# Flamingo attention and feed-forward block: the last query stack issued behind both sums, and the opening's splits and transfers put in another order

## The chip, the cores and the metric

The kernel runs on 1 core of one Trainium2 chip. Its time is the device time of one execution in microseconds (us), as the median of several runs. A core has five engines that run their own instruction streams in order: TensorE (PE, with its weight loads as PEld), VectorE (DVE), ScalarE (ACT), GpSimd (POOL) and SyncE (SP), which only issues transfers here. ACT issues transfers too, from the same stream as its computations. Semaphores are all that couples the streams.

## The reference, cut to what matters

64 sequences of 256 positions and 512 features, each on its own:

```python
def _L0_xattn_ref(q, k, v, ffn_w, ffn_b):      # q = layernorm(x), k = v = ctx
    qs = relu(q.reshape(bs, ts, 16, 32)); ks = relu(k...); vs = relu(v...)
    att = einsum('bthf,byhf->bhty', qs, ks)
    att = softmax(att / sqrt(32), axis=-1)
    out = einsum('bhty,byhf->bhtf', att, vs).reshape(bs, ts, -1)
    return relu(out @ ffn_w.T + ffn_b)
# _L0_ffn_ref: xr, xk mix x with x of the position before (mu_r, mu_k);
#   r = sigmoid(xr @ W_r); out = r * (square(relu(xk @ W_k)) @ W_v)
x = x + tanh(g_xattn) * _L0_xattn_ref(layernorm(x), ctx, ctx, ffn_w, ffn_b)
x = x + tanh(g_ffn)   * _L0_ffn_ref(layernorm(x), W_r, W_k, W_v, mu_r, mu_k)
```

## The kernel before

The 16 heads of a sequence are four groups c = 0 to 3 of four heads. Products are taken in fp32r from high and low halves: a value is split into a rounded part (ACT, `q_halve` L598, `k_halve` L603) and the rest (DVE, `q_low` L838, `k_low` L844). The halves of the queries and keys go to memory (`write_q` L558 on ACT's queue, `write_k` L263 on SP's) and come back stacked on 96 partitions, group by group (`stack_q` L573 on ACT, `stack_k` L283 on SP). A group's heads can be multiplied once both stacks have landed.

For each head PE makes `scores` (L1079, from which DVE takes the row maximum, `head_max` L858) and, with the maxima moved into a 97th row of `q_st` (`move_m` L295), `shifted_scores` (L1095), whose exponent ACT takes (`exponent` L618). For group 1 alone the denominators are not made by PE: ACT sums the exponents of the plain scores in the score bank itself (`sum_exp` L621, heads 4 to 7), and PE may write the next scores to that bank only behind it: `scores` of heads 7, 8 and 9 of a sequence wait for the sums of heads 5, 6 and 7. The attention output goes to memory (`write_o` L303) and back in another layout (`read_o` L309, tile `o_mv`, in two halves for each of two position tiles u); ACT and POOL split it (`o_high` L635, `o_low` L431) and PE multiplies it (`project` L1151). That is done for tile 0 at the end of an iteration, and for tile 1 in the next one.

Each engine has a function `iteration(i, par)` that writes out its order by hand: in iteration i the heads of sequence i, the projection and feed-forward layers of i-1 and i-2 between them, and the preparation of i+1 and i+2. `pipeline` runs i = -3 to 3 unrolled, a loop of two iterations a turn, and the last ones unrolled. Iterations -2, -1 and 0 of SP have an order of their own, `opening` (L330), since nothing is in the pipeline yet. There the weights are loaded and split as well. Sequence 0 has its group 0 written to memory by itself (`k_first`, `q_first`), so that its stack need not wait for the rest.

In ACT's `iteration` (L705) the second line is `stack_q(i, 3, par)`, behind `exponent(i, 0)` and ahead of `sum_exp(i, 6)`.

## Time and profile before

| | |
|---|---|
| median of 3 runs | 2684.31 us |
| lowest, highest | 2683.58, 2691.25 us |
| the profiled execution's own time | 2686.47 us |
| its span, first to last instruction | 2684.7 us |
| PE busy | 2597.9 us, 97% of the span |
| DVE, ACT, POOL busy | 85%, 63%, 43% |

So 1.77 us of the profiled execution lie outside its span. The page gives for each group of instructions its busy time, and the time its engine sat idle just before it with the one that ended that idle time (`<-`). Idle time of an engine that is not the bottleneck costs nothing. The span divides into an opening of some 130 us, 61 or so sequences at an even pace of about 40.4 us, and an ending.

### The profile page before, as it was taken

How to read it: one execution, taken by the hardware profiler on the slowest of the kernel's cores; microseconds unless marked ns; L12 is line 12 of the kernel's file. 1: busy time of each engine (PE TensorE's matmuls, PEld its weight loads, DVE VectorE, ACT ScalarE, POOL GpSimd, SP SyncE). 2: the span in 40 equal slices, each digit the busy share in tenths (PEclk: the TensorE clock that was granted, in tenths of full speed). 3: DMA queues.
4: the chain of work that ended last, by engine and by line, in shares of the span. 5: the costliest groups of instructions: out<-in, count | busy, mean ns of one | idle time of the engine just before them, and what ended most of it. 6: DMA issues, size and time to landing. Idle time of an engine off the chain costs nothing. (4 is left out here: it accounts for less than half of the span.)

```text
span 2684.7 us, 66755 instructions
## 1 busy us (share of the span) xinstructions
PE 2597.9 (97%) x20354; PEld 2074.9 (77%) x20354; DVE 2282.9 (85%) x4109; ACT 1695.4 (63%) x3531; POOL 1162.9 (43%) x902
## 2 busy tenths in 40 slices
PE   3799999999999999999999999999999999999998
PEld 2577778787787787787787778778778778787776
DVE  6688888888888889888888888888888888888875
ACT  4466666666666666666666666666666666666663
POOL 0144444444444444444444444444444444444434
PEclk9799999999999999999999999999999999999999
DMA  9787777777777778778778778787787787777751
GB/s 256 210 215 228 215 213 230 222 212 229 221 209 233 223 208 234 218 209 234 223 209 234 218 211 232 211 222 224 214 227 222 211 231 222 211 228 220 209 153 44
DMA packets 523216, 576.78 MB, mean 215 GB/s; under 512 B 191264, under 2 KB 422688, under 8 KB 523168
## 3 DMA queue, kind: packets, MB, share of 16 engines
q1 hardware_dynamic: 369648, 340.71, 46.5%
q10 hardware_dynamic: 153520, 235.46, 30.1%
q8 instruction: 26, 0.43, 0.1%
q14 instruction: 22, 0.18, 0.0%
HBM read 373.56 MB, written 201.33 MB: 214 GB/s over the span
## 5 line engine op out<-in xcount | busy, mean ns | idle before, releaser
L618 ACT ACTIVATE probs<-bank 128x512 f32<-128x512 f32 x1024 | 610.2, 596 | 523.2 <-PE bank L1103 519.7
L858 DVE TENSOR_REDUCE m_nat<-bank 128x2 fp32r<-128x512 f32 x1024 | 689.2, 681 | 76.5 <-PE bank L1091 76.3
L1091 PE MATMUL bank<-k_st,q_st 96*128 96x256 f32 x2048 | 435.1, 295 | 37.5 <-ACT bank L630 26.2
L877 DVE RECIPROCAL o_val<-bank 128x256 f32<-128x256 f32 x192 | 336.7, 1754 | 138.8 <-PE bank L1129 138.8
L1091 PEld LDWEIGHTS bank<-k_st,q_st 96*128 96x128 f32 x2048 | 362.8, 193 | 108.0 <-ACT bank L630 40.1
L1103 PE MATMUL bank<-q_st,k_st 97*128 97x256 f32 x2048 | 426.2, 290 | 8.6 <-DMA q_st<-m_t 8.2
L1103 PEld LDWEIGHTS bank<-q_st,k_st 97*128 97x128 f32 x2048 | 357.3, 191 | 85.5 <-issue 23.3
L464 POOL TENSOR_TENSOR xm<-xm 128x512 f32<-128x512 f32 x128 | 157.1, 1227 | 463.0 <-ACT xm L677 462.0
L630 ACT ACTIVATE bank<-bank,m_nat 128x256 f32<-128x256 f32 x512 | 227.6, 444 | 136.5 <-DVE m_nat L858 136.2
L431 POOL TENSOR_TENSOR o_lo<-o_mv,o_hi 128x512 fp32r<-128x512 f32 x128 | 168.6, 1317 | 304.5 <-ACT o_hi L640 302.1
L1146 PE MATMUL bank<-xk_hi,w_hi 128*128 128x256 f32 x1024 | 294.9, 288 | 1.0 <-DVE th L940 1.0
L1146 PE MATMUL bank<-xk_hi,w_lo 128*128 128x256 f32 x1024 | 288.3, 282 | 0.0
L1146 PE MATMUL bank<-xk_lo,w_hi 128*128 128x256 f32 x1024 | 288.1, 281 | 0.0
L1117 PE MATMUL bank<-probs,v_pos 128*32 128x256 f32 x4096 | 278.1, 390 | 0.0
L449 POOL TENSOR_TENSOR xk_lo<-xm,xk_hi 128x512 fp32r<-128x512 f32 x128 | 209.3, 1636 | 125.3 <-DVE xm L923 111.6
L423 POOL TENSOR_TENSOR rstd<-ve,mhalf 128x1 f32<-128x1 f32 x128 | 69.4, 542 | 415.2 <-DVE ve L907 415.2
L1146 PE MATMUL bank<-w_hi,o_hi 128*128 128x512 f32 x512 | 208.7, 408 | 2.3 <-POOL o_lo L431 2.1
L1146 PE MATMUL bank<-w_hi,xr_hi 128*128 128x512 f32 x512 | 207.9, 406 | 0.0
L1146 PE MATMUL bank<-w_hi,ka_hi 128*128 128x512 f32 x512 | 206.9, 404 | 0.0
L1129 PE MATMUL bank<-probs,ones_r 128*32 128x256 f32 x3072 | 203.6, 383 | 0.0
L1146 PE MATMUL bank<-w_lo,o_hi 128*128 128x512 f32 x512 | 203.2, 397 | 0.0
L1146 PE MATMUL bank<-w_hi,ka_lo 128*128 128x512 f32 x512 | 202.0, 394 | 0.0
(94 smaller groups left out, 5945.8 us busy)
## 6 DMA issues: line engine op xcount, KB each, us to landing
q_st<-q_dram ACTq DMA_DIRECT2D x256, 256.0 KB, 4.8
k_st<-k_dram SPq DMA_DIRECT2D x256, 256.0 KB, 4.7
k_raw<-ctx_t_dram SPq DMA_DIRECT2D x256, 128.0 KB, 5.1
q_st<-q_dram ACTq DMA_DIRECT2D x256, 128.0 KB, 2.9
k_st<-k_dram SPq DMA_DIRECT2D x256, 128.0 KB, 5.0
o_dram<-o_val SPq DMA_DIRECT2D x256, 128.0 KB, 2.1
o_mv<-o_dram SPq DMA_DIRECT2D x1024, 32.0 KB, 3.1
x<-x_dram ACTq DMA_DIRECT2D x64, 512.0 KB, 6.7
```

The costliest lines, as they stand in the source:

```text
L431: nc.gpsimd.tensor_tensor(by_tile(o_lo, u), o_mv[:, :, :].rearrange("p g (k a) -> p k g a", k=KC), by_tile(o_hi, u).bitcast(F32), ALU.subt ...
L449: nc.gpsimd.tensor_tensor(xk_lo[:, part, :], xm[:, part, :], xk_hi[:, part, :].bitcast(F32), ALU.subtract).then_inc(xk_lo_ready, 1)
L464: nc.gpsimd.tensor_tensor(part, part, part, ALU.mult).then_inc(ka_ready, 1)
L618: nc.scalar.activation(probs[:, n // GR % 2, n % GR, :, :].rearrange("p v t -> p (v t)"), st_bank[n % 2][:, :], ACT.Exp).then_inc(exp_read ...
L630: last = nc.scalar.activation(scores, scores, ACT.Exp, bias=m_nat[:, SUMMED % 2, g, u:u + 1].bitcast(F32), accum_out=den[:, NU * g + u:NU ...
L858: nc.vector.tensor_reduce(m_nat[:, c % 2, n % GR, :], s_bank[n % 2][:, :].rearrange("p (u y) -> p u y", u=NU), AX_X, ALU.max, negate=True) ...
L877: nc.vector.reciprocal(o_val[:, c % 2, :], pv_bank[:, T:2 * T]).then_inc(rden_ready, 1)
L1091: mm = nc.tensor.matmul(s_bank[n % 2][:, T * u:T * u + T], q_st[0:QK, c, g, P * u:P * u + P], k_st[0:QK, c, g, :], start=True, stop=True)
L1103: mm = nc.tensor.matmul(st_bank[n % 2][:, T * v:T * v + T], k_st[0:ST, c, g, P * v:P * v + P], q_st[0:ST, c, g, :], start=True, stop=True)
L1117: nc.tensor.matmul(pv_bank[HD * g:HD * g + HD, 0:T], v_pos[:, v, HD * h:HD * h + HD], probs[:, c % 2, g, v, :], start=(v == 0), stop=(v == ...
L1129: mm = nc.tensor.matmul(pv_bank[HD * g:HD * g + HD, T:2 * T], ones_r[:, 0:HD].bitcast(F32), moving, start=(n == 0), stop=(n == len(sums) - 1))
L1146: mm = nc.tensor.matmul(dst, lhs[a], rhs[c], start=first and n == 0, stop=last and n == 2, skip_group_check=True)
```

## The change

1. **All sequences.** `stack_q(i, 3)`, two transfers, moves on ACT from ahead of `sum_exp(i, 6)` to behind `sum_exp(i, 7)`.
2. **Sequence 0, splits.** The keys are split before the queries; the queries of group 0 are split in instructions of their own, and written as soon as these are through.
3. **Sequence 1, splits.** `k_halve(1)` moves from ACT's iteration -1 to iteration 0, behind `sum_exp(0, 6)`; `k_low(1)` on DVE to behind `head_max(0, 9)`.
4. **SP's opening.** Key writes and stacks move ahead of loads; the reads of `o_mv` are spread out, the second one ahead of `move_m(1, 0)`.

```diff
@@ SP: opening
                 if i == -2:
                     load_k(0)
                     load_w(range(0, 4))
+                    write_k_first(0, par)
                     load_x(1)
+                    stack_k(0, 0, par)
                     write_k(0, par)
                 elif i == -1:
-                    stack_k(0, 0, 1 - par)
                     stack_k(0, 1, 1 - par)
+                    stack_k(0, 2, 1 - par)
+                    move_m(0, 0)
                     load_k(1)
-                    move_m(0, 0)
-                    stack_k(0, 2, 1 - par)
                     load_x(2)
...
                     stack_k(1, 0, 1 - par)
+                    stack_k(1, 1, 1 - par)
                     load_k(2)
                     move_m(0, 3)
                     load_w(range(6, 7))
                     write_o(0, 0)
-                    stack_k(1, 1, 1 - par)
                     load_x(3)
+                    read_o(0, 0, 0)
                     write_o(0, 1)
                     stack_k(1, 2, 1 - par)
+                    read_o(0, 0, 1)
                     move_m(1, 0)
                     load_w(range(7, 8))
-                    read_o(0, 0, 0)
-                    read_o(0, 0, 1)
@@ ACT: write_q, sequence 0
+                        act.wait_ge(q_hi_first, 1)
+                        act.wait_ge(q_lo_first, 1)
                         for half, tile in enumerate((q_high, q_raw)):
                             act.dma_start(q_dram[par, 0, half].rearrange("f g t -> (f g) t"),
                                           tile[:, 0, :]).then_inc(q_first, 16)
+                    act.wait_ge(q_hi_ready, b + 1)
+                    act.wait_ge(q_lo_ready, b + 1)
@@ ACT: iteration
+                if isinstance(i, int) and i == -2:
+                    k_halve(i + 2)
...
                 exponent(i, 0)
-                stack_q(i, 3, par)
                 sum_exp(i, 6)
+                if isinstance(i, int) and i == 0:
+                    k_halve(i + 1)

                 exponent(i, 1)
                 split_high(i, 6, 1)
                 sum_exp(i, 7)
+                stack_q(i, 3, par)
@@ DVE: iteration
                 head_max(i, 9)
+                if isinstance(i, int) and i == 0:
+                    k_low(i + 1)
                 stats_1(i + 2)
...
                 norm_1(i + 2)
+                if isinstance(i, int) and i == -2:
+                    k_low(i + 2)
```

What this does to the streams, at three places. ACT in iteration 1 and all later ones, before: the two transfers `q_st<-q_dram` of group 3 stand behind the first exponent (L618), ahead of the sums (L630) of heads 6 and 7; after them L677 clears a bank.

```order
L640 ACTIVATE o_hi<-o_mv 128x4x128
L630 ACTIVATE bank,den<-bank,m_nat 128x256 x2
L618 ACTIVATE probs<-bank 128x512
L580 DMA q_st<-q_dram 32x1024
L581 DMA q_st<-q_dram 64x1024
L630 ACTIVATE bank,den<-bank,m_nat 128x256 x2
L618 ACTIVATE probs<-bank 128x512
L630 ACTIVATE bank,den<-bank,m_nat 128x256 x2
L618 ACTIVATE probs<-bank 128x512
```

The same stretch of ACT now:

```order
L653 ACTIVATE o_hi<-o_mv 128x4x128
L643 ACTIVATE bank,den<-bank,m_nat 128x256 x2
L631 ACTIVATE probs<-bank 128x512
L643 ACTIVATE bank,den<-bank,m_nat 128x256 x2
L631 ACTIVATE probs<-bank 128x512
L643 ACTIVATE bank,den<-bank,m_nat 128x256 x2
L587 DMA q_st<-q_dram 32x1024
L588 DMA q_st<-q_dram 64x1024
L631 ACTIVATE probs<-bank 128x512
```

Both transfers moved past two sums and one exponent. SP at the end of its opening, before, from the weights `th` on (L300 moves the maxima, L307 writes the attention output, L315 reads it back, eight transfers in one go):

```order
L241 DMA th<-w_v_dram 128x2x512
L307 DMA o_dram<-o_val 128x256
L289 DMA k_st<-k_dram 64x1024
L291 DMA k_st<-k_dram 32x1024
L252 DMA x_ln<-x_dram 16x2x512 x8
L307 DMA o_dram<-o_val 128x256
L289 DMA k_st<-k_dram 64x1024
L291 DMA k_st<-k_dram 32x1024
L300 DMA q_st<-m_t 1x8x128
L241 DMA xn<-w_v_dram 128x2x512
L315 DMA o_mv<-o_dram 32x4x64 x8
```

The same stretch of SP now:

```order
L243 DMA th<-w_v_dram 128x2x512
L311 DMA o_dram<-o_val 128x256
L254 DMA x_ln<-x_dram 16x2x512 x8
L319 DMA o_mv<-o_dram 32x4x64 x4
L311 DMA o_dram<-o_val 128x256
L295 DMA k_st<-k_dram 64x1024
L297 DMA k_st<-k_dram 32x1024
L319 DMA o_mv<-o_dram 32x4x64 x4
L304 DMA q_st<-m_t 1x8x128
L243 DMA xn<-w_v_dram 128x2x512
```

The key stack of sequence 1, group 1, left this stretch for an earlier place, and all of `o_mv` now stands ahead of the maxima's row `q_st<-m_t`. SP at its start, before, from the key load of sequence 0 on:

```order
L260 DMA k_raw<-ctx_t_dram 32x4x256 x4
L241 DMA probs<-w_x_dram 128x2x512 x2
L241 DMA x<-w_r_dram 128x2x512 x2
L252 DMA x_ln<-x_dram 16x2x512 x8
L272 DMA k_dram<-k_high 128x256
L272 DMA k_dram<-k_raw 128x256
L275 DMA k_dram<-k_high 128x3x256
L275 DMA k_dram<-k_raw 128x3x256
L289 DMA k_st<-k_dram 64x1024
L291 DMA k_st<-k_dram 32x1024
```

The same stretch of SP now:

```order
L262 DMA k_raw<-ctx_t_dram 32x4x256 x4
L243 DMA probs<-w_x_dram 128x2x512 x2
L243 DMA x<-w_r_dram 128x2x512 x2
L279 DMA k_dram<-k_high 128x256
L279 DMA k_dram<-k_raw 128x256
L254 DMA x_ln<-x_dram 16x2x512 x8
L295 DMA k_st<-k_dram 64x1024
L297 DMA k_st<-k_dram 32x1024
L271 DMA k_dram<-k_high 128x3x256
L271 DMA k_dram<-k_raw 128x3x256
```

Group 0 of the keys goes out ahead of the load of x of sequence 1 (`x_ln`), and is stacked ahead of the other groups' writes.

## Rows read from the trace of the kernel before

**Rows 1.** The page: span, and its section 1, busy us, share, instructions.

```profile
span 2684.7 us, 66755 instructions
...
PE 2597.9 (97%) x20354; PEld 2074.9 (77%) x20354; DVE 2282.9 (85%) x4109; ACT 1695.4 (63%) x3531; POOL 1162.9 (43%) x902
```

**Rows 2.** Waits of PE, 140 to 2600 us: us in total, times, longest.

```profile
PE bank L1091 <- ACT bank L630: 15.9, 61, 0.3
...
PE bank L1146 <- POOL o_lo L431: 0.5, 1, 0.5
```

**Rows 3.** Timeline, one sequence: start, us, engine, line, op, out<-in, shapes, [idle<-releaser].

```profile
1014.84 0.44 ACT L630 ACTIVATE bank<-bank,m_nat 128x256 f32<-128x256 f32 x1
...
1015.86 0.36 ACTq L580 DMA_DIRECT2D q_st<-q_dram  x1
...
1015.91 0.50 PE L1091 MATMUL bank<-k_st,q_st 96*128 96x256 f32 x2 [0.26 <-ACT bank L630]
...
1016.88 0.45 ACT L630 ACTIVATE bank<-bank,m_nat 128x256 f32<-128x256 f32 x1 [0.51 <-DVE m_nat L858]
...
1020.78 0.40 PE L1091 MATMUL bank<-k_st,q_st 96*128 96x256 f32 x2
...
1021.57 0.21 ACT L630 ACTIVATION_READ_ACCUMULATOR bank<-bank,m_nat 128x1 f32 x1
...
1021.97 0.41 PE L1091 MATMUL bank<-k_st,q_st 96*128 96x256 f32 x2
```

**Rows 4.** The output write at 1021.5: duration ns, start; its landing, us.

```profile
L307 SPq DMA_DIRECT2D o_dram<-o_val x1: 344/344/344, 1021.5 to 1021.5; - x1
...
DMA to landing us min/median/max: 1.7/1.7/1.7
```

**Rows 5.** The output write at 101.3, issued among a query stack's two transfers.

```profile
L307 SPq DMA_DIRECT2D o_dram<-o_val x1: 343/343/343, 101.3 to 101.3; - x1
...
DMA to landing us min/median/max: 2.3/2.3/2.3
```

**Rows 6.** Stretch: us, PE, PEld, DVE, ACT, POOL busy, PEclk, DMA share, GB/s.

```profile
1021.00:1024.00 3.00, 3.00 (x27) 3.00 (x26) 2.98 (x8) 2.47 (x7) 0.67 (x1) 1.00 0.35 96
1024.00:1029.00 5.00, 5.00 (x34) 4.57 (x33) 4.70 (x12) 3.13 (x5) 2.48 (x3) 1.00 0.89 270
```

**Rows 7.** Timeline of POOL and PE at the projection of tile 1, two sequences.

```profile
1030.30 1.44 POOL L431 TENSOR_TENSOR o_lo<-o_mv,o_hi 128x512 fp32r<-128x512 f32 x1 [1.58 <-ACT o_hi L640]
...
1032.23 0.48 PE L1146 MATMUL bank<-w_hi,o_hi 128*128 128x512 f32 x1
...
1353.94 1.28 POOL L431 TENSOR_TENSOR o_lo<-o_mv,o_hi 128x512 fp32r<-128x512 f32 x1 [1.75 <-ACT o_hi L640]
...
1355.37 0.47 PE L1146 MATMUL bank<-w_hi,o_hi 128*128 128x512 f32 x1
```

**Rows 8.** Timeline of the opening, sequence 0: ACT and PE.

```profile
14.07 1.04 ACT L607 ACTIVATE k_high<-k_raw 128x1024 fp32r<-128x1024 f32 x1
...
28.06 1.19 PE L1091 MATMUL bank<-k_st,q_st 96*128 96x256 f32 x4 [2.99 <-DMA k_st<-k_dram]
...
37.06 0.80 PE L1091 MATMUL bank<-k_st,q_st 96*128 96x256 f32 x2 [4.20 <-ACT bank L630]
...
47.75 0.80 PE L1103 MATMUL bank<-q_st,k_st 97*128 97x256 f32 x2 [2.17 <-DMA q_st<-m_t]
```

**Rows 9.** Timeline of the opening, start of sequence 1: PE and ACT.

```profile
68.39 0.77 PE L1091 MATMUL bank<-k_st,q_st 96*128 96x256 f32 x2 [4.57 <-DMA k_st<-k_dram]
...
76.37 0.80 PE L1103 MATMUL bank<-q_st,k_st 97*128 97x256 f32 x2 [2.55 <-DMA q_st<-m_t]
76.97 1.05 PE L1042 MATMUL bank<-w_hi,ident_r 128*128 128x512 f32 x2
...
79.63 0.63 ACT L640 ACTIVATE o_hi<-o_mv 128x512 fp32r<-128x512 f32 x1 [5.40 <-DMA o_mv<-o_dram]
...
81.22 0.80 PE L1091 MATMUL bank<-k_st,q_st 96*128 96x256 f32 x2 [3.20 <-ACT bank L630]
```

**Rows 10.** Timeline of SP's issues in the same stretch.

```profile
61.74 0.52 SPq L289 DMA_DIRECT2D k_st<-k_dram  x1
...
62.95 5.37 SPq L252 DMA_DIRECT2D x_ln<-x_dram  x8
...
73.14 0.69 SPq L300 DMA_DIRECT2D q_st<-m_t  x1
...
74.35 3.79 SPq L315 DMA_DIRECT2D o_mv<-o_dram  x8
```

More of the change, by code:

```diff
@@ L145, in flamingo_block @@
         q_copied = sem("q_copied")
+        q_hi_first = sem("q_hi_first")
+        q_lo_first = sem("q_lo_first")
         q_first = sem("q_first")
@@ L266, in write_k @@
                     sp.wait_ge(k_lo_ready, b + 1)
-                    groups = slice(0, CH)
-                    if first_sequence(b):
-                        groups = slice(1, CH)
-                        for half, tile in enumerate((k_high, k_raw)):
-                            sp.dma_start(k_dram[par, 0, half].rearrange("f g t -> (f g) t"),
-                                         tile[:, 0, :]).then_inc(k_first, 16)
+                    groups = slice(1 if first_sequence(b) else 0, CH)
                     for half, tile in enumerate((k_high, k_raw)):
@@ L276, in write_k, with write_k_first @@
                                      tile[:, groups, :]).then_inc(k_written, 16)
+            def write_k_first(b, par):
+                sp.wait_ge(k_hi_ready, b + 1)
+                sp.wait_ge(k_lo_ready, b + 1)
+                for half, tile in enumerate((k_high, k_raw)):
+                    sp.dma_start(k_dram[par, 0, half].rearrange("f g t -> (f g) t"),
+                                 tile[:, 0, :]).then_inc(k_first, 16)
             def keys_written(b):
@@ L288, in stack_k @@
                         sp.wait_ge(k_first, 32)
+                    if first_sequence(b) and c == 1:
+                        sp.wait_ge(k_written, 32)
                     sp.dma_start(k_st[0:2 * HD, c, :, :].bitcast(F32),
@@ L291, in stack_k @@
                     sp.dma_start(k_st[2 * HD:QK, c, :, :].bitcast(F32), k_dram[par, c, 0]).then_inc(k_stacked[c], 16)
-                    if first_sequence(b) and c == 0:
-                        sp.wait_ge(k_written, 32)
             def move_m(b, c):
@@ L600, in q_halve @@
                     act.wait_ge(q_copied, NU * (b + 1))
-                    nc.scalar.activation(q_high[:, :, :].bitcast(F32R), q_raw[:, :, :], ACT.Copy).then_inc(q_hi_ready, 1)
+                    groups = slice(0, CH)
+                    if first_sequence(b):
+                        groups = slice(1, CH)
+                        nc.scalar.activation(q_high[:, 0, :].bitcast(F32R), q_raw[:, 0, :],
+                                             ACT.Copy).then_inc(q_hi_first, 1)
+                    nc.scalar.activation(q_high[:, groups, :].bitcast(F32R), q_raw[:, groups, :],
+                                         ACT.Copy).then_inc(q_hi_ready, 1)
             def k_halve(b):
@@ L762, in iteration @@
                 xt_copy(i - 1, 1)
-                k_halve(i + 2)
+                if not (isinstance(i, int) and i < 0):
+                    k_halve(i + 2)
                 exponent(i, 11)
@@ L1005, in iteration @@
                     q_low(i + 2)
-                k_low(i + 2)
+                if not (isinstance(i, int) and i < 0):
+                    k_low(i + 2)
                 split_low(i, 4, 0)
```

12 lines of the change are left out of this document (8 added, 4 removed).

## The prediction

> **What bounds the kernel now.** I read the page first: the span is 2684.7 us and PE is busy for 2597.9 us of it, 97% [rows 1]. PE is the bound, so an edit counts only where it moves PE. Next the waits of PE over the even-paced part, 140 to 2600 us. Only one group is of note: 61 waits, one a sequence, for a sum on ACT, 15.9 us together or 0.26 us each; the projection waits for POOL once in all that time [rows 2]. So the even-paced part has at most some 16 us to give, and only if the edit touches that one wait. The rest of PE's idle time lies in the opening, where single waits reach 4.57 us [rows 8, 9]. I followed both places in the timeline.
>
> **The wait in the loop, and which sum it is.** The reader is to match the two L630 stretches of one sequence with PE. The sum at 1014.84 is head 5's, ahead of the exponent; PE's scores of head 7 start at 1015.91 as it ends, with the 0.26 us of idle time. The query stack is issued at 1015.86, behind it. The sum that follows the stack, head 6's, starts at 1016.88, and what waits for it (scores of head 8) runs at 1020.78, 2.9 us after that sum is through (1016.88 plus twice 0.45, and its readout). Head 7's sum ends at 1021.78 (1021.57 + 0.21) and head 9's scores start at 1021.97; but this sum stands behind exponent 1, which waits for PE itself, not behind the stack [rows 3]. So the moved stack blocked none of PE's waits: its two issues cost ACT some 0.3 us ahead of head 6's sum, all of it covered by 2.9 us. **Gain of the move in the loop: 0.** That the 15.9 us stay is my first claim.
>
> **What the moved stack now meets.** It is issued about 5.5 us later, at about 1021.4 instead of 1015.86, while head 7's sum runs [rows 3]. On ACT the two issues (0.36 us and about 0.5 us) run beside that sum's tail; the exponent of head 2 behind them comes at most 0.5 us later, and PE asks for it only two heads on. Its landing has room: group 3 is not multiplied until head 12, three heads behind head 9's scores. Cost on ACT: 0. But in memory traffic it now falls beside the write of the attention output of group 3, issued at 1021.5. That write begins a chain: it lands in 1.7 us [rows 4], `o_mv` is read back, ACT makes `o_hi`, POOL `o_lo`, PE projects. In the sequence shown POOL is through at 1031.74 (1030.30 + 1.44) and PE projects at 1032.23, a room of 0.49 us. In another it is through at 1355.22 and PE projects at 1355.37: 0.15 us is the signal alone, there is no room [rows 7]. Over the 59 sequences that I measured so, 9 have no room, the median is 0.66 us. A delay of the last `o_mv` by d costs PE what is left of d: summed over these rooms (less the 0.15 us), 0.3 us of delay would cost some 3.5 us in all, 0.5 us some 9 us, 0.8 us some 19 us.
>
> How large is d? The nearest row from above is the same write at 101.3, issued among the two transfers of a query stack: 2.3 us instead of 1.7 [rows 5], 0.6 us late. From below: the traffic has a hole just there, a DMA share of 0.35 in 1021 to 1024, 1.95 us of free time, against 0.89 behind it [rows 6]. The stack's 393 kB need 1.3 us at the 303 GB/s of a full share (270 GB/s at 0.89); so it fits, and adds nothing, if it falls well. SP has the output of x to issue before it reads `o_mv` back, which hides another 0.1 to 0.2 us of the write. I take d = 0.2 us, nearer to the hole, since the end of the chain hangs on the traffic of 1024 to 1029, which the hole shields: 9 sequences at 0.2 us, and 0.3 us from the rest: **+2.1 us**. The ends are 0 and +9 us (d = 0.5).
>
> On this the Trainium skill has a rule that speaks against the change: DMA: Bandwidth & Descriptors, section Queues, rings and completion order, says that each DMA engine takes turns between the queues that have work, a packet at a time. By that rule the stack on ACT's queue would take every second turn from the write on SP's and slow it as in rows 5; by the hole it would not. It is the second rival below.
>
> **The opening, step by step.** It is a row of gates; a gain ahead of a gate counts only if the gate moves too.
> First gate: group 0 of sequence 0 is multiplied at 28.06, when the key stack lands. The keys were split last, at 14.07 and without any wait for them [rows 8]; now they are split while ACT and DVE wait for x, so the write goes out some 5 us sooner, and the stack lands 4 to 6 us sooner. The query side comes 1.5 us sooner too, by the short first split (a quarter of the elements). Price: x of sequence 1 is loaded 2 us later and its query copy stands ahead of the stack of queries of group 1, so group 1 wins 1 us at most. PE's wait at 37.06 for a sum (4.20 us) came from the splits of sequence 1's keys on ACT and DVE; both are gone from there: about 2.5 us sooner.
> Second gate, 47.75: the maxima's row of group 1 [rows 8]. On SP it stands behind the load of x of sequence 2, and that behind the key load, which now is issued later. I find it 0.5 to 1 us sooner; 1.5 to 2 us of the win are lost. The later `k_low(1)` moves the writes of sequence 1's keys by at most 1 us either way.
> Third: 68.39, 4.57 us of waiting for the key stack of group 1, issued at 61.74 [rows 9, 10]. It now stands right behind group 0's, 6 us sooner. This wait goes, 4 us. What is late next is the gate at 76.37, the maxima's row issued at 73.14. SP's queue before it, from 61.7: 5.4 for x (without the stack ahead of it it starts 1.2 us sooner), 1.9 for four `o_mv` issues (half of 3.79), 0.4 and 1.1 for write and stack, then the second read has to wait for the write issued at about 69.0 to land (1.7 us in the loop [rows 4]; up to 6 us in this traffic, in which the stack of 61.74 was needed at 68.39 and had not come before), and 1.9 for its four issues: 72.6 to 76.9, against 73.14. I take 3 us for the landing, 73.9 in all: this gate is 0.8 us *later*, at 77.2, and the 4 us are lost.
> Fourth: 81.22, PE waits 3.20 us for a sum, which stood behind `o_high`, which waited for `o_mv` until 79.63 [rows 9]. The reads end with SP at 72.6 to 76.9 instead of 78.14 (74.35 + 3.79), so this is 1.2 to 5.5 us sooner and with the 73.9 no longer binds; what does is PE itself: 77.2 plus 1.7 us (76.37 to 78.02, the two L1042 products included) is 78.9. **So the opening gives 81.22 - 78.9 = 2.3 us; with the earlier signals a little more, -2.5 us.** Ends: the row of maxima could be late by 3.8 us, which turns the gain into a loss of 0.7 us, or early by 0.5 us, which gives 3.6 us; to that up to 1 us either way for what the first gates hand on: +1 to -5 us. Behind 81.22 the order is the old one and I expect the gain to be carried to the end, since PE works without a break from 130 us on.
>
> **Sum**, against the span of 2684.7 us: -2.5 + 2.1 = -0.4, 2684.3 us. The profiled execution took 2686.47 us, 2.2 above the median of 2684.31. On the median it is 2684.31 - 0.4 = **2683.9 us**. About 0.3%, 8 us, is what a measurement of this kernel can tell from no change.
>
> **Rivals.**
> 1. *The chain to the projection breaks in most sequences (slower).* The stack takes the place in the traffic that `o_mv` had, d = 0.8 us or more; PE then waits at L1146 for POOL in 35 or more of 61 sequences: +19 us at 0.8 us, +27 at 1.0. With the opening 2684.3 - 2.5 + 19 = 2701. For it: ACT waits for `o_mv` in every sequence already. Against it: the hole of 1.95 us [rows 6]. It decides from d = 0.6 us on. Chance 0.10.
> 2. *The two queues take turns.* The write lands 0.6 us late as in rows 5, SP's other issue hides 0.1 us, d = 0.5 us: 2684.3 + 8.7 - 2.5 = 2690.5. The skill's rule of turns, named above, is this case. Chance 0.17.
> 3. *The opening gives nothing.* The maxima's row of sequence 1 is the gate and comes 2 us or more late, since two reads now stand before it. With the 2.1 us: 2686.4. Chance 0.17.
> 4. *The opening's gains carry through*: the gate at 76.37 does not come later, and the 3.20 us, the 4.57 us and 2 us from the first gates are all kept: 2684.3 - 9.8 = 2674.5. Against it: SP's queue. Chance 0.11.
> 5. The forecast, 2681 to 2686: chance 0.45.
>
> **Numbers.** The range has to leave out no more than 2 in 10: from 2678, which cuts most of rival 4, to 2693, which takes in rival 2 with 3 us above it and leaves rival 1. Faster by over 0.3% is below 2676.3: most of rival 4, 0.09. Slower is above 2692.4: rival 1 and a quarter of rival 2, 0.14. The rest, 0.77, is within.
>
> **What the profile after would show.** Right: 61 waits of PE for ACT's sums, 16 us in all, as before; waits of L1146 for POOL in about ten sequences, 1 to 4 us in all; the opening with no wait near 68 us, one near 73 to 77 us for the row of maxima of 3 us or more, and the third `exponent` stage some 2.5 us sooner. Wrong: if the 15.9 us shrink, my reading of which sum PE waits for is false; if waits at L1146 come to 8 us or more, d is mis-sized; if sequence 2 starts more than 5 us or less than 0 us sooner, my SP queue is.

## The result: slower, and the profile after

Seven runs of each kernel on one chip: the changed kernel 2697.49 us (2692.67 to 2701.94), the kernel before 2688.44 us (2679.15 to 2693.47). The ratio is 1.0038, 95% interval 1.002 to 1.0055: **slower by 0.4%, some 10 us of 2688** (9.1 us between the medians), where I had forecast no change, 2683.9 us, and a range that ended at 2693. The forecast was wrong, and what happened is its first rival. On another chip the same kernel gave 2695.77 against 2685.3, ratio 1.003 (1.0018 to 1.0043).

The page after: span and the busy lines of section 1, to be set against [rows 1].

```profile
span 2700.2 us, 66759 instructions
...
PE 2601.9 (96%) x20354; PEld 2076.5 (77%) x20354; DVE 2282.7 (85%) x4110; ACT 1689.4 (63%) x3532; POOL 1156.6 (43%) x902
```

PE has the same 20354 products and 4 us more of busy time in a span 15.5 us longer. So it waits more. These are two single executions, 15.5 us apart where the medians are 9.1 apart; a part of the difference is explained below. The waits of PE from 140 to 2600 us (us in total, times, longest), against [rows 2]:

```profile
PE bank L1120 <- ACT bank L643: 15.5, 60, 0.3
PE bank L1175 <- POOL o_lo L436: 12.5, 24, 1.1
PE bank L1132 <- DMA q_st<-m_t: 0.8, 1, 0.8
```

The first line is the wait that a reader would have wanted the move to shorten. It was 15.9 us in 61 waits and is 15.5 in 60: untouched. The second was 0.5 us, once; now the projection waits for POOL in 24 sequences. Of the waits before, one line of the same view did not stand ahead of the prediction, and matters now: PE's turning of the maxima (L1058) waited for DVE.

```profile
PE bank L1058 <- DVE m_t L867: 4.5, 9, 0.6
```

After, that line is gone: as I read it, a PE that has just waited for POOL finds the maxima ready. So 12.0 us came in and 4.5 us were given back. All lines of this view together are 21.3 us before and 29.0 after, +7.7 us. DVE takes the reciprocals of a sequence's first denominators once a sequence (tile `rden`), and I use the start of that as the sequence's mark: from mark 3 to mark 60 the kernel before takes 2308.5 us, the changed one 2318.8, +10.3 us. The opening, up to mark 3, is 0.9 us longer, the rest behind mark 60 is 4.2 us longer.

Two parts of this are not waits in that view. Between the marks PE's busy time is 2.9 us longer (2288.4 and 2291.3 us), with the same 18127 products at the full clock; what draws it out is not shown. And behind mark 60 most of the 4.2 us is the clock's. The columns of this row are those of [rows 6]; PEclk, the third number from the end, is the granted clock, and 0.50 is the lower of PE's two levels, 1.2 GHz.

```profile
2658.50:2665.30 6.80, 6.19 (x15) 4.87 (x16) 4.40 (x7) 1.76 (x5) 3.33 (x3) 0.50 0.00 0
```

PE had stood idle for 3.27 us, until 2659.11, waiting for POOL's half of the output, and the clock fell in that wait. Products of 512 columns then follow each other at 0.43 us, and at 0.24 once the clock is back, so PE's 6.19 us there cost some 2.8 us, an estimate. The wait itself is 1.7 us longer than the longest for POOL in the ending before (1.6 us). The profile before has no such stretch until its last 1.1 us, behind PE's last product, and the second profile of the changed kernel, on the other chip (span 2694.7 us), none behind mark 60 until its last 0.2 us.

**The chain that now sets PE.** ACT and its queue (ACTq) in the sequence that answers to [rows 3]; columns are start, duration, engine, line, operation, out<-in, and in brackets the idle time ahead and its releaser. The exponent of head 1 is L631, the sums are L643, the moved stack L587 and L588.

```profile
1025.26 0.60 ACT L631 ACTIVATE probs<-bank 128x512 f32<-128x512 f32 x1 [2.71 <-PE bank L1132]
1025.52 0.33 ACTq L587 DMA_DIRECT2D q_st<-q_dram  x1
1025.75 0.45 ACT L643 ACTIVATE bank<-bank,m_nat 128x256 f32<-128x256 f32 x1
1025.88 0.51 ACTq L588 DMA_DIRECT2D q_st<-q_dram  x1
```

The stack stands behind the sum of head 7 in the code, yet its first transfer is issued 0.23 us before that sum starts, while the exponent of head 1 still runs. SP's queue in the same sequence, and the landing of its output write (to be set against [rows 4]):

```profile
1026.45 0.34 SPq L311 DMA_DIRECT2D o_dram<-o_val  x1
...
1029.72 1.85 SPq L319 DMA_DIRECT2D o_mv<-o_dram  x4
```

```profile
L311 SPq DMA_DIRECT2D o_dram<-o_val x1: 343/343/343, 1026.5 to 1026.5; - x1
...
DMA to landing us min/median/max: 3.2/3.2/3.2
```

So the stack goes out 0.93 us *ahead* of the write, whose landing takes 3.2 us instead of 1.7, and the read, which waits for that landing, is issued 3.27 us behind the write. What follows, on ACT, POOL and PE, against [rows 7]:

```profile
1035.86 0.63 ACT L653 ACTIVATE o_hi<-o_mv 128x512 fp32r<-128x512 f32 x1 [2.17 <-DMA o_mv<-o_dram]
...
1036.57 1.27 POOL L436 TENSOR_TENSOR o_lo<-o_mv,o_hi 128x512 fp32r<-128x512 f32 x1 [2.39 <-ACT o_hi L653]
...
1037.99 0.47 PE L1175 MATMUL bank<-w_hi,o_hi 128*128 128x512 f32 x1 [0.71 <-POOL o_lo L436]
```

ACT stands idle for 2.17 us until `o_mv` is there, POOL's second half is through at 1037.84, and PE, 0.71 us idle, starts 0.15 us behind it, which is the signal alone. The traffic shows the same: the hole of [rows 6], a DMA share of 0.35 in the 3 us up to the read of the tile, is filled to 0.71 (us, busy time of PE, PEld, DVE, ACT, POOL, then the granted clock, the DMA share, GB/s):

```profile
1026.00:1029.00 3.00, 3.00 (x27) 3.00 (x26) 3.00 (x8) 2.46 (x7) 0.68 (x1) 1.00 0.71 187
1029.00:1034.00 5.00, 5.00 (x34) 4.57 (x33) 4.70 (x13) 3.13 (x5) 2.32 (x3) 1.00 0.83 260
```

The trace also records the packets of each queue: their number, MB, and share of the 16 engines' time. In the sequence above, 1027 to 1028 has packets of ACT's queue (q10) alone, though SP's write was issued at 1026.45; in 1028 to 1029 both queues have some.

```profile
q10 hardware_dynamic: 44, 0.11, 62.4%
```

```profile
q10 hardware_dynamic: 56, 0.17, 46.5%
q1 hardware_dynamic: 128, 0.12, 33.4%
```

The write is 128 packets of 1 KB, the stack 96 of 4 KB. Before, the write's packets start 0.84 to 1.31 us behind its issue (medians of the 59 sequences 3 to 61); in the change 1.66 to 2.71, with 53 of the stack's packets ahead of the first and 43 between the first and the last. So of the 1.4 us that the last one is late, 0.8 is a later start of the first, while the engines were not full (62.4%), and 0.6 a slower run among the stack's packets. What holds the first one back is not shown.

I measured this chain in 59 sequences (3 to 61) of each profile. All times below are medians in us from the issue of the output write; "no room" counts the sequences in which PE projects within 0.16 us of POOL's end. The kernels of the other rows are explained in the next section; the row behind the first sum is the one with the old opening.

| kernel | stack issued | stack landed | write landed | read issued | last `o_mv` landed | no room |
|---|---|---|---|---|---|---|
| before | -5.6 | -1.1 | 1.74 | 1.98 | 7.82 | 9 |
| small transfer moved | -5.6, -1.0 | 1.4 | 1.83 | 1.98 | 7.89 | 15 |
| stack behind the first sum | -4.8 | 0.7 | 1.79 | 1.98 | 8.10 | 15 |
| large transfer moved | -5.6, -1.0 | 2.4 | 2.81 | 2.88 | 8.48 | 36 |
| stack behind both sums | -0.9 | 2.9 | 3.12 | 3.18 | 8.54 | 42 |
| the change | -0.9 | 2.9 | 3.12 | 3.18 | 8.66 | 39 |
| stack behind the write | 0.8 | 5.1 | 1.74 | 1.98 | 9.82 | 59 |

**The opening after**, the products with the idle time of PE ahead of them; they answer to [rows 8] and [rows 9].

```profile
26.10 1.20 PE L1120 MATMUL bank<-k_st,q_st 96*128 96x256 f32 x4
...
34.96 0.80 PE L1120 MATMUL bank<-k_st,q_st 96*128 96x256 f32 x2 [3.19 <-ACT bank L643]
...
46.88 0.80 PE L1132 MATMUL bank<-q_st,k_st 97*128 97x256 f32 x2 [2.40 <-DMA q_st<-m_t]
...
79.14 0.80 PE L1132 MATMUL bank<-q_st,k_st 97*128 97x256 f32 x2 [9.29 <-DMA q_st<-m_t]
...
80.59 0.67 PE L1120 MATMUL bank<-k_st,q_st 96*128 96x256 f32 x2
```

The first scores came 2.0 us sooner (28.06 before; there PE waited for the keys, here it goes from a product of its own to the scores), the gate at 37.06 2.1 us sooner, the one at 47.75 0.9. The wait of 4.57 us at 68.39 is gone, and PE waits 9.29 us for the row of maxima, until 79.14 instead of 76.37. SP's queue tells why, against [rows 10]:

```profile
61.74 5.11 SPq L254 DMA_DIRECT2D x_ln<-x_dram  x8
67.16 3.11 SPq L319 DMA_DIRECT2D o_mv<-o_dram  x4
70.31 0.43 SPq L311 DMA_DIRECT2D o_dram<-o_val  x1
70.78 0.51 SPq L295 DMA_DIRECT2D k_st<-k_dram  x1
71.33 0.58 SPq L297 DMA_DIRECT2D k_st<-k_dram  x1
75.50 1.74 SPq L319 DMA_DIRECT2D o_mv<-o_dram  x4
77.29 0.70 SPq L304 DMA_DIRECT2D q_st<-m_t  x1
```

SP stands still from 71.91 to 75.50, until the write of 70.31 has landed, 5.2 us after its issue. The row of maxima, free of that read, stands behind it.

### The profile page after: what moved, and what is told of

Its sections match the earlier page's. It is cut to its first block and busy times, and to the rows that moved or that the text cites. A ratio compares the mean times of both kernels' runs of the same rounds, so it can differ in the third digit from the quotient of the medians.

```text
span 2700.2 us, 66759 instructions
## 1 busy us (share of the span) xinstructions
PE 2601.9 (96%) x20354; PEld 2076.5 (77%) x20354; DVE 2282.7 (85%) x4110; ACT 1689.4 (63%) x3532; POOL 1156.6 (43%) x902
## 5 line engine op out<-in xcount | busy, mean ns | idle before, releaser
L631 ACT ACTIVATE probs<-bank 128x512 f32<-128x512 f32 x1024 | 609.1, 595 | 508.7 <-PE bank L1132 504.4
L643 ACT ACTIVATE bank<-bank,m_nat 128x256 f32<-128x256 f32 x512 | 227.1, 444 | 116.5 <-DVE m_nat L882 116.5
L1175 PE MATMUL bank<-w_hi,o_hi 128*128 128x512 f32 x512 | 209.0, 408 | 16.3 <-POOL o_lo L436 15.8
L1175 PE MATMUL bank<-w_hi,o_lo 128*128 128x512 f32 x512 | 202.5, 396 | 0.0
```

The source lines that it names most:

```text
L631: nc.scalar.activation(probs[:, n // GR % 2, n % GR, :, :].rearrange("p v t -> p (v t)"), st_bank[n % 2][:, :], ACT.Exp).then_inc(exp_read ...
L643: last = nc.scalar.activation(scores, scores, ACT.Exp, bias=m_nat[:, SUMMED % 2, g, u:u + 1].bitcast(F32), accum_out=den[:, NU * g + u:NU ...
L1175: mm = nc.tensor.matmul(dst, lhs[a], rhs[c], start=first and n == 0, stop=last and n == 2, skip_group_check=True)
```

## Experiments

Theory: the moved stack delays the output write, and with it the read of `o_mv` and the projection. Rivals: the opening costs the 10 us; or any delay of the stack costs something, wherever it ends. Each kernel was timed against the kernel before on the same chip, 5 to 12 runs against 25 to 29. What was expected stands under each heading as it was written ahead of the run.

### The loop's move alone

The kernel before with one line moved.

```diff
                 exponent(i, 0)
-                stack_q(i, 3, par)
                 sum_exp(i, 6)
...
                 sum_exp(i, 7)
+                stack_q(i, 3, par)
```

> Only the query stack of group 3 is moved behind both sums; the opening is as before. Theory 1 (the stack's traffic delays the attention output's write, and with it the projection): the loss is here. The write issued beside the stack lands 3.1 us after its issue instead of 1.7, PE waits for POOL's o_lo in 20 to 30 sequences, 10 to 15 us, and the time is 10 to 14 us above before. Theory 2 (the loss comes from the opening, by a row of maxima that waits behind two reads, and by a phase of the loop that it leaves behind): within 3 us of before, and the write at 1.7 us.

Measured: 2694.87 us against 2687.01, ratio 1.0036 (1.0022 to 1.005). Waits of PE, 140 to 2600 us:

```profile
PE bank L1091 <- ACT bank L630: 15.4, 60, 0.3
PE bank L1146 <- POOL o_lo L431: 9.2, 16, 1.3
```

The same new wait, and the whole loss within the intervals. The move in the loop is the cause. Here too the waits in the view are not all of it: 25.0 us together, 3.7 above before, in a loop that is 7.3 us longer from mark 3 to mark 60.

### The opening alone

The changed kernel with that line moved back.

```diff
                 exponent(i, 0)
+                stack_q(i, 3, par)
                 sum_exp(i, 6)
...
                 sum_exp(i, 7)
-                stack_q(i, 3, par)
```

> The changed opening, with the query stack of group 3 where it was before. Theory 1: sequences 3 and on keep the pace of before; the opening gives or costs less than 1.5 us, PE still waits some 9 us near 70 to 79 us for the row of maxima; time within 2 us of before, and PE waits for o_lo 1 to 3 us in all. Theory 2: 8 to 14 us above before.

Measured: 2688.87 against 2687.01, ratio 1.0012 (1.0003 to 1.0021). No new wait for POOL (0.2 us). But no gain either; the opening is taken up again below.

### The distance from the write: between the sums

The changed kernel with the stack between `sum_exp(i, 6)` and `exponent(i, 1)`, 4.8 us ahead of the write.

> The changed kernel with the stack of group 3 behind the first of the two sums only: it is issued some 3.5 us ahead of the output's write instead of 0.9 us. Theory 1: at that distance the traffic is through before the write starts; the write lands in 1.7 to 1.9 us, no more waits for o_lo than before (under 3 us), and the time is that of the kernel with the changed opening alone. If instead what costs is that the stack lies behind a sum at all (ACT's stream, a later landing of the stack), it is 5 us or more slower than that one.

Measured: 2684.91 against 2687.01, ratio 0.9995 (0.9986 to 1.0004). Its waits, same stretch:

```profile
PE bank L1120 <- ACT bank L643: 15.7, 60, 0.3
PE bank L1087 <- DVE m_t L891: 1.4, 3, 0.5
PE bank L1175 <- POOL o_lo L436: 0.6, 3, 0.3
```

The wait for POOL is gone again although the stack is still later than before. What counts is not that it is late but what it meets. The same place in the kernel before, opening untouched:

```diff
                 exponent(i, 0)
-                stack_q(i, 3, par)
                 sum_exp(i, 6)
+                stack_q(i, 3, par)
```

> The kernel before with its opening untouched; the last query stack of every sequence is issued between the two sums instead of ahead of both. Theory 1 (what costs is a query transfer that is in flight when the attention-output write is issued, because the write then lands with it): with the stack issued 4.8 us ahead of the write and landed 0.6 us behind it, the write still lands after 1.7 us, the last read of attention outputs lands 8.1 us behind the write, some 17 of 59 sequences have no room, and the time is that of before within 1 us or 2 to 3 us below it, as the loop of the earlier kernel with this place was 3.3 us shorter than before. Theory 2 (any later place costs in proportion to how much later it is): 0.8 of the 4.7 us moved, so +1 to +2 us. Theory 3 (the shorter loop of the earlier kernel only paid back its slow opening): within 1 us of before.

Measured: 2681.9 against 2684.61, ratio 0.9988 (0.9977 to 1.0). Theory 1 held; the size of the gain, 0 to 3 us, stays at the edge of what can be told.

### One transfer of the two

`stack_q` issues a 128 KB and a 256 KB transfer. The kernel before, with only the larger one moved:

```diff
                 exponent(i, 0)
-                stack_q(i, 3, par)
+                stack_q_part(i, 3, par, 0)
                 sum_exp(i, 6)
...
                 sum_exp(i, 7)
+                stack_q_part(i, 3, par, 1)
```

> The kernel before with only the 256 KB transfer of the stack moved behind both sums, the 128 KB one stays. Theory 1, with the delay given by the bytes in front of the write: two thirds of the traffic, the write lands at 2.4 to 2.8 us, waits for o_lo of 4 to 8 us, time 4 to 8 us above before. If the delay comes from the end of the last transfer issued ahead of it whatever its size: the write at 3 us, and the full 10 to 14 us.

Measured: 2688.36 against 2687.01, ratio 1.0002 (0.999 to 1.0014). The write lands at 2.81 and there is no room in 36 sequences, yet it costs next to nothing: its waits of 140 to 2600 us are 7.2 us for POOL, 15.8 for ACT's sums and none for DVE, 23.2 in all, only 1.9 above before (in its profile the loop is 3.4 us longer).

```profile
PE bank L1101 <- ACT bank L639: 15.8, 61, 0.3
PE bank L1156 <- POOL o_lo L431: 7.2, 14, 1.7
```

So the delay of the last `o_mv` does not by itself give the size of the loss: it is 0.66 us here and 0.72 with both transfers moved, and the two kernels took 2688.36 and 2694.87 us on the same chip. What makes that difference is open.

Only the smaller one moved (parts 1 and 0 exchanged):

> The kernel before with only the smaller of the stack's two transfers (128 KB) moved behind both sums; the 256 KB one stays ahead of them. Moving the 256 KB one alone held the write until 2.8 us, put the last read of attention outputs at 8.5 us behind the write, and cost some 1.4 us in the timed runs against 7.4 for both. Theory A (the write lands with whatever query transfer is in flight at its issue): 128 KB issued 0.9 us ahead of it is done about 1.4 us behind it, so the write lands at 1.8 to 2.2 us, the last read at 7.9 to 8.3 us, and the time is within 2 us of before. Theory B (both transfers cost alike by being late, whatever is behind them): the write at 1.74, the last read as late as with the large one, 8.4 us or more, +2 to +5 us.

Measured: 2686.96 against 2684.12, ratio 1.0013 (1.0002 to 1.0024). The landing of the write, one sequence:

```profile
L307 SPq DMA_DIRECT2D o_dram<-o_val x1: 343/343/343, 1061.7 to 1061.7; - x1
...
DMA to landing us min/median/max: 1.8/1.8/1.8
```

As theory A has it, 1.83 us in the median: the stack has landed 1.4 us behind the write's issue, within the 1.7 us that the write takes anyway. In the table the write always lands at its own 1.7 us or 0.2 to 0.5 us behind the stack that went ahead of it, whichever is later. The time does not follow in this pair: it sits 0.1% above before, with 4.0 us of waits for POOL, and the trace does not account for those 2.8 us.

### Behind the write

If a stack ahead of the write is what delays it, one place more should free the write. The kernel before with the stack behind `exponent(i, 2)`:

```diff
                 exponent(i, 0)
-                stack_q(i, 3, par)
                 sum_exp(i, 6)
...
                 exponent(i, 2)
+                stack_q(i, 3, par)
```

> The kernel before with the last query stack of every sequence issued later still, behind the third exponent, so 0.5 to 1 us BEHIND the issue of the attention-output write instead of 0.9 us ahead of it. Theory 1 (the write waits for the query transfer ahead of it, and the read of attention outputs waits for the write): the write lands after 1.7 to 2.2 us again and the read is issued at 2.0 to 2.4 us; the stack then competes with the read itself, so that the last of it lands 8.0 to 8.4 us behind the write, half of the loss at most, +1 to +4 us. Rival (the total of bytes asked for in that stretch decides, not the order): the last read lands at 8.6 us or later, as with the stack ahead of the write, and the time is +7 us or more. Rival (queues take turns and 393 kB beside the 524 kB read cost the whole 1.3 us): the last read at 9.1 us, and more than +10 us.

Measured: 2784.45 against 2684.61, ratio **1.0371** (1.0346 to 1.0396), +100 us. The write is free again, as expected:

```profile
L307 SPq DMA_DIRECT2D o_dram<-o_val x1: 344/344/344, 1057.0 to 1057.0; - x1
...
DMA to landing us min/median/max: 1.7/1.7/1.7
```

Yet PE now waits for POOL in every sequence or nearly so. Its waits, 140 to 2600 us:

```profile
PE bank L1146 <- POOL o_lo L431: 64.0, 56, 3.1
PE bank L1091 <- ACT bank L630: 15.2, 58, 0.3
PE bank L1091 <- DMA q_st<-q_dram: 7.4, 15, 0.7
```

I expected +1 to +4 us and missed by far. The stack, issued 0.8 us behind the write, now goes ahead of the *read* (issued at 1.98), and pushes ACT's load of `v_pos` behind it from 1.1 to 2.1 us behind the write, beside the read as well. The last `o_mv` lands 2.0 us later than before. I take both cases for one: what goes out just ahead of a link of the chain write, read, split, project makes that link longer. Which of the two transfers beside the read does it was not separated. The three waits above and one small one come to 86.8 us, 65.5 above before, in a loop 87.1 us longer. PE's busy time between the marks is 22.3 us longer, and 20.5 us of that loop run at 1.2 GHz, in six stretches of 3.4 us, where the kernel before has none: up to 10 us by my estimate. How ACT's wait for `o_mv` grows shows it in one line each, total us and times in 140 to 2600 us, before:

```profile
  DMA o_mv<-o_dram: 60.9, 56
```

with the stack between the sums (and the new opening), in the change, and behind the write:

```profile
  DMA o_mv<-o_dram: 72.8, 57
```

```profile
  DMA o_mv<-o_dram: 82.4, 60
```

```profile
  DMA o_mv<-o_dram: 145.3, 59
```

### The opening: the row of maxima first

The opening alone with two lines of SP exchanged:

```diff
-                    read_o(0, 0, 1)
                     move_m(1, 0)
+                    read_o(0, 0, 1)
                     load_w(range(7, 8))
```

> The change's opening alone, with the move of sequence 1's first row of maxima put ahead of the second read of attention outputs in SyncE's queue, so that it no longer waits for the output write (landed after 5.2 us in the changed kernel). If that wait is what took the opening's gain: the row is moved some 5 us sooner than 77.3 us, the 9.3 us wait of TensorE that ended at 79.1 us ends at 75 to 76.5 us, the mark of sequence 1 is 2.5 to 4 us ahead of before instead of 0.4 to 1, and the time is 1.5 to 3.5 us below the opening alone. If something else ends that wait (the rows' own computation, or the query stack), the mark moves by less than 1 us, and if later waits of the opening take it back, the mark of sequence 1 is sooner and that of sequence 3 is not.

Measured: 2681.84 against 2684.61, ratio 0.9989 (0.9979 to 0.9999). The row goes out without the wait, and PE's gate ends sooner (SP, then PE):

```profile
71.17 0.70 SPq L304 DMA_DIRECT2D q_st<-m_t  x1
```

```profile
75.65 0.80 PE L1132 MATMUL bank<-q_st,k_st 97*128 97x256 f32 x2 [4.13 <-DMA q_st<-m_t]
```

That looked like a gain of 6 us over the opening alone. It was not one. The opening alone timed again on another chip, and the row first again on a third:

> The change's opening alone once more, the row of maxima behind the second read of attention outputs as in the change, to be timed on the same chip as the kernels with the row first. If the row's place is worth 3 to 6 us as two calls of runs suggest (ratio 1.0012 with it behind, 0.9989 with it ahead), this is +1 to +4 us against before. If the difference was the chip's, it is 0 to 3 us below before. The single loss of some 4.6 us between the marks of sequences 3 and 4 in the earlier profile belongs to the kernel if it is there again, and to that execution if not.

> The opening with the row first, stack at its old place, once more. Ratio 0.9989 before. If that was the kernel's, 0.998 to 0.9995 again; if it was the chip's, 1.000 to 1.001, as the opening with the row behind (1.0012 and 1.0005).

Measured: 2686.25 against 2684.12, ratio 1.0005 (0.9996 to 1.0015), and 2687.93 against 2685.3, ratio 1.001 (0.9998 to 1.0022). In the whole change:

```diff
 the changed kernel
-                    read_o(0, 0, 1)
                     move_m(1, 0)
+                    read_o(0, 0, 1)
```

> The whole change, last query stack behind both sums, with only the row of maxima put ahead of the second read of attention outputs. If the two losses add (loop +7 to +8 us as in the kernel with the stack's move alone, opening -2.5 to -3.5 us as in the kernel with the row first): +4 to +5.5 us against before, 2 to 4 us below the changed kernel, marks of sequences 1 to 3 ahead of before by 2.5 to 3.5 us and lost again by sequence 20. If the change's loss beyond the stack's move (2.6 us) is not the opening's, the time is that of the changed kernel, +9 us or more. If the opening's gain is swallowed by the longer loop altogether, +7 us.

> The changed kernel with the row of maxima ahead of the second read. If the row's place is worth the 3 us of the earlier profile, 3 us below the changed kernel; if it is worth nothing, within 2 us of it; if it does harm where the stack is late (1.0056 before), 4 to 6 us above it.

> The changed kernel as it is, once more, beside its variant with the row of maxima first. Ratio to before 1.0038 when first timed. If that loss is the stack's move (1.0036 alone) and the opening is worth nothing: 1.003 to 1.005 again, +8 to +13 us; the write lands after 3.1 us and the last read of attention outputs 8.5 to 8.8 us behind it.

Measured: 2700.71 against 2684.12, ratio 1.0056 (1.004 to 1.0071); the same kernel again 2694.46 against 2685.3, ratio 1.0028 (1.0016 to 1.004); on that chip the change as it is 2695.77, ratio 1.003 (1.0018 to 1.0043). So one kernel gave 1.0056 and 1.0028, another 0.9989 and 1.001, on different chips: ratios taken on different chips that differ by less than some 0.3% don't tell two kernels apart, however narrow each interval is. Where both ran on the same chip, the row's place changes nothing (1.0028 and 1.003).

The first sequence's queries halved whole again, in the opening with the row first:

```diff
-                        act.wait_ge(q_hi_first, 1)
-                        act.wait_ge(q_lo_first, 1)
+                        act.wait_ge(q_hi_ready, b + 1)
+                        act.wait_ge(q_lo_ready, b + 1)
...
                     groups = slice(0, CH)
-                    if first_sequence(b):
-                        groups = slice(1, CH)
```

> The opening of the change with the row of maxima ahead of the second read of attention outputs, but the first sequence's queries halved whole again, not by group. If the split by group is what brings the first gates forward: the first scores, 26.1 us with it and 28.1 us before, start at 26.8 to 28.1 us, and the marks of sequences 1 to 3, 2.6 to 3.5 us ahead of before with the split, are 0.5 to 2 us ahead. If the gain is all the transfers' order on SyncE: the marks of sequences 1 to 3 stay 2.5 to 3.5 us ahead. Time: that of the kernel with the split, or 1 to 2 us above it.

Measured: 2685.24 against 2684.12, ratio 1.0003 (0.9994 to 1.0012): not to be told from the kernel with the split. In its profile the first scores start at 26.59 us (28.06 before, 26.10 in the change), so most of that gain comes without the split of the queries. Mark 1 is at 92.8 us and mark 3 at 180.8, some 5 us behind the kernels with the split; that is a single profile and not to be built on.

What the times can't tell, the marks of the other profiles can in part, at sequences 1 and 3. The rows are the reciprocals of the first denominators (L886 before, L910 after) of sequence 1: before, the change, and the opening alone in its second profile.

```profile
93.39 0.20 DVE L886 RECIPROCAL rden<-den 128x8 f32<-128x8 f32 x1
```

```profile
92.38 0.20 DVE L910 RECIPROCAL rden<-den 128x8 f32<-128x8 f32 x1
```

```profile
90.02 0.19 DVE L910 RECIPROCAL rden<-den 128x8 f32<-128x8 f32 x1
```

| opening | profiles | mark 1, mean (lowest, highest) | mark 3, mean (lowest, highest) | PE idle up to mark 1 | at 1.2 GHz up to mark 1 | at 1.2 GHz from mark 1 to 3 |
|---|---|---|---|---|---|---|
| before | 6 | 93.7 (92.7, 95.0) | 177.0 (176.1, 178.0) | 50.2 | 24.4 | 16.6 |
| the change's | 5 | 91.2 (88.5, 93.0) | 178.0 (176.3, 180.5) | 50.8 | 19.6 | 20.7 |
| the change's, row first | 6 | 91.2 (89.9, 92.6) | 175.7 (174.1, 176.9) | 48.0 | 21.5 | 18.3 |

The last three columns are means in us.

At mark 1 the opening is 2.5 us ahead, and at mark 3 it has lost it all and 1 us more. By my estimate most of both is the clock's. Up to mark 1 PE is idle no less than before (50.8 and 50.2 us), but 4.8 us less of the time is granted at 1.2 GHz, worth up to 2.4 us if half of such time is lost; from mark 1 to mark 3 it is 4.1 us more, worth up to 2.1 of the 3.5 us lost. With the row first PE is idle 2.1 us less up to mark 1. Whether the order of transfers moved these stretches of low clock or they fell so by chance is not shown. A part of the loss is a wait, as one pair of rows suggests: PE's gate at the next row of maxima of sequence 1, in the opening alone (second profile) and with the row first.

```profile
91.05 0.80 PE L1132 MATMUL bank<-q_st,k_st 97*128 97x256 f32 x2 [4.23 <-DMA q_st<-m_t]
```

```profile
87.16 0.79 PE L1132 MATMUL bank<-q_st,k_st 97*128 97x256 f32 x2 [0.47 <-DMA q_st<-m_t]
```

With the row first 1.3 us of the gain are left at mark 3 in the mean. That is 0.05% of the time, and no timing here could show it.

### Both findings in one kernel

Row first, and the stack between the sums, timed on two chips.

```diff
 the changed kernel
                     write_o(0, 1)
                     stack_k(1, 2, 1 - par)
-                    read_o(0, 0, 1)
                     move_m(1, 0)
+                    read_o(0, 0, 1)
...
                 sum_exp(i, 6)
+                stack_q(i, 3, par)
...
                 sum_exp(i, 7)
-                stack_q(i, 3, par)
```

> The same order in the opening, with the last query stack between the two sums. Theory 1 and the opening's wait together: the loop like that of the kernel with the stack between the sums (no loss, up to 3 us gain), the opening 2 to 3 us ahead of before, so 2682 to 2686 us beside 2687 for before. If the loop only pays back what the opening loses, the gain of the opening is gone by the end and the time is that of before within 1 us.

> The opening with the row first and the stack between the sums, once more. Ratio 0.9984 before. If it is a gain, 0.9975 to 0.9993 again with its interval below 1; if it was the chip's, 0.9995 to 1.0005.

Measured: 2680.76 against 2684.61, ratio 0.9984 (0.9976 to 0.9993), and 2682.88 against 2685.3, ratio 0.9987 (0.9978 to 0.9996). It beats the kernel before by 2.4 to 3.9 us in the medians, and the changed kernel by about 13 us on the second chip (2682.88 against 2695.77). All four timings with the stack between the sums have a ratio below 1, and both of this kernel have their interval below 1. A single kernel's ratio moved by 0.2 to 0.3% between chips, so a gain of 0.15% rests on these timings agreeing and not on any one interval. Where it comes from was not separated; in its second profile PE's waits of 140 to 2600 us are 20.7 us against 21.3 before.

## Why the prediction was wrong, point by point

- **What bounds the kernel, and which sum PE waits for: right.** 15.9 us before, 15.5 after, 15.2 to 16.0 in every experiment, wherever the stack stood. The rooms of POOL ahead of PE have a median of 0.60 us, not the 0.66 of the text; the sums over them are as stated.
- **The moved stack's issue: the time was off, and it mattered.** I read it as 1021.4 beside a write at 1021.5, 0.1 us ahead of it. It is 0.94 us ahead in the median, since ACT issues it while the exponent of head 1 still runs. That put all its 393 kB in front of the write.
- **The delay d: the step that failed.** I took 0.2 us, and 0 to 0.5 as its ends; measured are 0.84 us in the change and 0.72 with the move alone (8.66 and 8.54 less 7.82). Two errors make it. The upper bound came from a write that had one of the stack's transfers ahead of it and landed after 2.3 us [rows 5]; here both were ahead and it took 3.1. And the hole of [rows 6] was counted as free room for the bytes, as if only throughput counted. It did take them, but the write also stands in that hole, and the chain waits for its landing: its first packet started 1.66 us behind the issue instead of 0.84, its last 2.71 instead of 1.31.
- **The price of d: right in kind, too high in size.** The sum over the rooms gives 20.7 us at 0.84 (19 at 0.8 in the text). POOL's wait grew by 12.0 us, and 4.5 us came back where PE used to wait for DVE, which the sum did not know; the loop lost 10.3 us. Why POOL's wait grew by 12.0 and not by 20.7 is open. At d = 2.0 the same sum gives 81 us and POOL's wait grew by 63.5; that profile is 93.6 us longer, in part by the clock, of which the sum knows nothing.
- **Rival 1 was the case** ("the stack takes the place in the traffic that `o_mv` had", 35 or more sequences, deciding from 0.6 us): 39 of 59 have no room, though the view shows a wait for POOL in only 24. I gave it 0.10 on the strength of the hole. Its 2701 was near to the 2697.49 that was measured, partly by two errors of opposite sign: 19 for 10 in the loop, -2.5 for nothing in the opening.
- **The rule of turns** was the second rival, with d = 0.5: the direction held, the size did not, since the write lands 0.2 us behind the end of the stack (2.9 and 3.12). The Trainium skill, DMA: Bandwidth & Descriptors, section Queues, rings and completion order, says that each DMA engine takes turns between its queues and drains a whole packet of several descriptors before it changes. The trace agrees in part: 43 of the stack's 96 packets start between the write's first and its last. That the write's first one starts 0.8 us late, while the engines are not full (62.4% in the sequence shown), is not explained by turns; and whether the trace's packets are those of the section is not shown.
- **The opening: the wait at 68.39 went, as said, and the row of maxima was the next gate, as said; its hour was wrong.** Predicted issue 73.9, measured 77.29: the first four `o_mv` issues took 3.11 us instead of 1.9, and the write landed after 5.2 us instead of 3, which is the 3.4. The gate ended at 79.14 instead of 77.2 and scores that I put at 78.9 came at 80.59. Over five profiles the lead at mark 1 is nevertheless 2.5 us, the number of the forecast, but by luck: PE is idle as long as before up to there, and what is less is the time at 1.2 GHz, 19.6 us instead of 24.4, which the forecast left out. The sentence behind it failed too, that behind 81.22 the order is the old one and the gain is carried: it is gone at mark 3. So "the opening gives nothing" (rival 3) was true of the time, and its reason only of half of it.
- **Numbers.** The sum was -2.5 + 2.1. Measured: about nothing for the opening (+0.9 us at mark 3 in the profile, ratios 1.0012 and 1.0005 alone) and +10 for the loop (+7.9 when the move was timed alone). The range left out rival 1 at 2701 on purpose; with a bound of 0.8 us for d it would have had to take it in.

## What to carry to other kernels

When a transfer is moved, list what is issued within its landing time around its new place, on *all* queues. If one of those is a link in a chain (write, wait, read, compute), ask what the chain loses when that link lands late. Idle bandwidth in the stretch (a share of 0.35) was no shelter here for a small transfer that something waited for. The place that did no harm, and gained 0 to 3 us, was the one from which the stack had landed ahead of the write's own landing, 4.8 us ahead of the write's issue; one place later cost 10 us and two places 100. A gain in an opening is to be followed by marks through the next sequences, with the granted clock beside them, before it is counted, and a gain of a tenth of a per cent is to be timed on more than one chip.

## What the runs showed of the hardware that was not expected

- A write of 128 KB on SP's queue, issued 0.94 us behind 393 kB on ACT's queue, lands after 3.12 us instead of 1.74 (medians of 59); issued 0.8 us ahead of the same 393 kB it lands after 1.74. Its first packet starts 1.66 us behind the issue in the first case and 0.84 in the second.
- A transfer on ACT's queue was issued at 1025.52, 0.23 us before the sum that stands ahead of it in ACT's stream started, and 0.26 us into the exponent ahead of that.
- Two profiles of one and the same kernel differ by 4 us at mark 1 (92.38 and 88.45 in the change), by 1 us at mark 3, and by 5.5 us at the end (spans 2700.2 and 2694.7). The granted clock goes with it: up to mark 1 it is at 1.2 GHz for 21.2 and 15.4 us, and in the ending the first one has a stretch of 6.8 us at that level which the second one has not.
